# Odd transpose sets of the probabilities written to the output projection's PSUM bank, and one residual moved up in VectorE's order

## The chip, the cores and the metric
The kernel runs on one core of a Trainium2 chip. The metric is the time of one execution on the device in microseconds (us), median of several runs. Engines: TensorE (PE in the profile; its weight loads are PEld), VectorE (DVE), ScalarE (ACT), GpSimd (POOL), and SyncE (SP), which issues the DMAs. PSUM is `ps`, eight banks of 128 partitions by 512 fp32.

## The reference, cut to what matters
A layer norm of 2048 tokens of 128 features feeds two branches whose outputs are added to the input. One is a linear attention with a short convolution, done once. The other, nearly all of the time, has six layers; each is a windowed attention and a gated feed-forward part:

```python
for i in range(DEPTH):      # 6
    x = attn_layer(shift_tokens(x), Wqkv[i], q_scale[i], k_scale[i], Wo[i]) + x
    x = ffn_layer(shift_tokens(x), ln_g[i], ln_b[i], W1[i], b1[i], W2[i], b2[i]) + x
```

The attention has 16 heads of 64, l2-normed and rotated queries and keys, windows of 32 queries that see 64 keys, a softmax, and `out @ Wo`. The feed-forward part normalizes, computes two products with W1, multiplies one with the gelu of the other, and applies W2. `shift_tokens` makes half of the features come from the token before.

## The kernel before, in words
The tokens are cut into groups of 256, so that six layers by eight groups make 48 steps. Every step runs parts of three groups at once: `a_` parts (projections, norms and rotation of group m), `b_` parts (scores, softmax, attention of group m - 1) and `c_` parts (second output projection, feed-forward of group m - 2). All engines follow one list, `SCHEDULE` (L57): `run` (L75) goes through it once per step, and an engine executes the tokens that it has a part for. What one engine needs of another is a semaphore wait at the head of a part. Within an engine the order of the list is the order of the queue. From that list, around the change:

- TensorE: ... c_mu b_s3 c_var a_x2 a_y2 b_pt0 b_pt1 b_att0 b_att1 a_sp0 c_h0 a_sp1 b_wo a_x3 c_h1 b_pt2 a_y3 b_pt3 b_att2 c_h2 a_norm1 b_att3 c_down
- VectorE: ... b_scale1 b_max1 c_zn a_mx2 a_my2 b_sum1 a_kn0 c_hm0 a_kn1 a_mx3 c_hm1 a_my3 c_hm2 c_fin b_xb, then b_rcq and a_mx0 of the next step
- ScalarE: ... c_rs a_rh a_sqy2 b_pto0 c_zh b_pto1 a_sqx2 b_exp1 b_oto0 c_gelu0 c_gelu1 b_pto2 a_sqy3 a_sqx3 (in the last group of a layer the split of the next layer's weights) b_pto3 c_gelu2 b_oto1
- POOL: ... b_sub1 a_xl c_zl b_nrm1 a_rot2 a_rot3
- SyncE: per step the windows of V, the keys (L317, after a_kn1), the queries (L329, after a_rot3), the halo.

The probabilities of one group are two chunks of 128 tokens by 16 heads. `b_pt(n, i)` (L551) transposes one of four sets, four 128 by 128 transposes (L564) into bank `PTB`; `b_pto` (L1083) on ScalarE copies the bank into `PT`; `b_att(n, i)` (L567) multiplies with V. All four sets use the same bank, so each waits for the copy of the one before (`pts_done`).

Bank `WO` holds in turn: the output projection of chunk 0 (`b_wo`, L594), read by the residual `b_xb` (L892); in the next step that of chunk 1 (`c_wo`), read by `c_xb`; the centred activations (`c_mu`, L600), read by `c_zsq` and by `c_zn` (L898) on VectorE; and the variance. `out_proj` (L581) waits before it writes the bank: for `zn_done` with chunk 0, for `xb_done` with chunk 1. The next scores, `b_s(n, 0)` (L511), wait for the queries' DMA (`q_in`). Of the feed-forward part, `c_h(0)` (L608) waits for `zl_done` from POOL.

Of the kernel before, what the change touches and what calls it, by code (L numbers as in the profile page):

```python
# [17 lines left out]
P = 128  # L18
# [4 lines left out]
C = T // P  # L23
# [11 lines left out]
HQ = 4  # L35
# [18 lines left out]
PTB, WO, NORM, FF = 4, 5, 6, 7  # L54
# [4 lines left out]
    a_norm0 a_xl+1 w_h1 a_sqx1 b_exp0 c_xs c_zl a_rck c_mu w_l0 b_s3 c_var b_nrm1 c_zsq a_halo a_x2 a_lnk a_rot2  # L59
    c_rs a_rot3 a_y2 a_rh a_sqy2 b_pt0 b_pto0 b_scale1 b_pt1 c_zh b_att0 w_l2 b_max1 b_att1 a_sp0 b_pto1 a_sqx2  # L60
    c_h0 c_zn b_exp1 a_mx2 a_sp1 a_my2 b_oto0 c_gelu0 b_sum1 b_wo a_x3 c_wl c_gelu1 a_kn0 b_pto2 c_h1 b_pt2 c_hm0
    a_y3 a_kn1 a_mx3 a_sqy3 a_sqx3 b_pt3 c_hm1 c_wh b_att2 c_h2 a_norm1 w_h2 a_my3 c_hm2 b_att3 b_pto3 c_down
    c_gelu2 c_fin b_xb w_l1 b_oto1""".split()
LAG = {"w": 0, "a": 0, "b": 1, "c": 2}
EARLY = """a_xs0 a_xh0 a_xl0 a_halo0 a_v0 a_vs0 a_v1 a_vs1 a_x0 a_y0 a_mx0 a_my0 a_sqy0 a_sqx0 a_rot0
    a_x1 a_y1 a_mx1 a_my1 a_sqy1 a_sqx1 a_rot1 a_norm0 a_sum0 a_rck0 a_lnk0 a_rh0 a_rl0 a_sp0 a_sp1 a_kn0 a_kn1
# [65 lines left out]
def program(nc, a):  # L132

    with ExitStack() as ctx:
        def sb(name, shape, dt=F32):
            return ctx.enter_context(nc.sbuf_tensor(name, shape, dt))

        def sem(name):
            return ctx.enter_context(nc.semaphore(name))

        ps = ctx.enter_context(nc.psum_tensor("ps", [P, 8, 512], F32))
# [31 lines left out]
        E = sb("E", [P, C, HP, 2, KEYS])  # L173
        PT = sb("PT", [P, HP, P])
# [16 lines left out]
        ident = sb("ident", [P, P])  # L191
# [49 lines left out]
        s = {name: sem(name) for name in SEMS}  # L241
# [137 lines left out]
        def _(e):  # L379
            def mm(out, lhsT, rhs, start=True, stop=True, **kw):  # L380
                return e.matmul(out, lhsT, rhs, start=start, stop=stop, **kw)  # L381
# [9 lines left out]
            for g in range(G1):  # L391
                for c in range(C1):
                    e.wait_ge(s["xn_done"], g * C1 + c + 1)
                    ins = e.transpose(ps[:, g, c * P:(c + 1) * P], xn[:, g * C1 + c, :], ident[:, :])
# [156 lines left out]
            def b_pt(n, i):  # L551
                c = i // 2
                if i % 2 == 0:
                    e.wait_ge(s["pn_done"], n * C + c + 1)
                if n or i:
                    e.wait_ge(s["pts_done"], n * 4 + i)
                for h in range(HQ):
                    if i == 0 and h == 1:
                        e.wait_ge(s["e_done"], n * C + C)
                    if i == 1 and h == HQ - 1:  # L560
                        e.wait_ge(s["v2_in"], n * 256 + 256)
                    if i == 2 and h == 1:
                        e.wait_ge(s["ots_done"], n * 4 + 2)
                    ins = e.transpose(ps[:, PTB, h * P:(h + 1) * P], E[:, c, i % 2 * HQ + h, :, :], ident[:, :])  # L564
                ins.then_inc(s["pt_done"], 1)

            def b_att(n, i):  # L567
# [13 lines left out]
            def out_proj(n, c):  # L581

                if c == 0 and n % G == 0:
                    e.wait_ge(s["wo_in"], n // G * 16 + 16)
                if c:
                    e.wait_ge(s["xb_done"], n * C + 1)
                elif n:
                    e.wait_ge(s["zn_done"], n)
                e.wait_ge(s["ots_done"], n * 4 + 2 * c + 2)
                for h in range(HP):  # L590
                    ins = mm(ps[:, WO, 0:P], wo[:, h, :], OT[:, c, h, :], h == 0, h == HP - 1)
                ins.then_inc(s["wo_done"], 1)

            def b_wo(n, _):  # L594
                out_proj(n, 0)

            def c_wo(j, _):
                out_proj(j, 1)
# [77 lines left out]
            def m_out(g):  # L676
# [4 lines left out]
                for c in range(C1):  # L681
# [30 lines left out]
            m_out(3)  # L712

            run({"a_v": a_v, "a_x": a_x, "a_y": a_y, "a_norm": a_norm, "a_sp": a_sp, "b_rqt": b_rqt, "b_s": b_s, "b_pt": b_pt,
                 "b_att": b_att, "b_wo": b_wo, "c_wo": c_wo, "c_mu": c_mu, "c_var": c_var, "c_h": c_h,
                 "c_down": c_down}, tail)
# [238 lines left out]
        def _(e):  # L955
            def act(out, in_, f=ACT.Copy, **kw):
                return e.activation(out, in_, f, **kw)  # L957
# [125 lines left out]
            def b_pto(n, i):  # L1083
                e.wait_ge(s["pt_done"], n * 4 + i + 1)
                if i % 2 == 0 and (i or n):
                    e.wait_ge(s["o_done"], n * C + i // 2)
                act(PT[:, i % 2 * HQ:i % 2 * HQ + HQ, :], ps[:, PTB, :]).then_inc(s["pts_done"], 1)

            def b_oto(n, c):
                for i in range(2):  # L1090
# [39 lines left out]
            def m_den(g):  # L1130
                e.wait_ge(s["dn_done"], g + 1)
                if g:
# [18 lines left out]
            a_sqx(0, 2)  # L1151
            run({"w_h": w_h, "c_wh": c_wh, "a_xs": a_xs, "a_xh": a_xh, "a_halo": a_halo, "a_vs": a_vs, "a_sqy": a_sqy, "a_sqx": a_sqx,
                 "a_lnk": a_lnk, "b_lnq": b_lnq, "a_rh": a_rh, "b_exp": b_exp, "b_pto": b_pto, "b_oto": b_oto, "c_xs": c_xs,
                 "c_zsq": c_zsq, "c_rs": c_rs, "c_zh": c_zh, "c_gelu": c_gelu}, lambda g: None)

# [129 lines left out]
```

## Time and profile before

| what | us |
|---|---|
| median of 3 runs | 1779.91 (1777.05 to 1782.78) |
| the profiled execution's own time | 1762.38 |
| its span, first to last instruction | 1760.6 |
| TensorE matmuls, weight loads | 1601.1 (91%), 1298.7 (74%) |
| VectorE, ScalarE, POOL | 1228.2 (70%), 1153.2 (65%), 1003.2 (57%) |
| mean granted TensorE clock | 0.983 |

A busy share is a mean over the whole span. Matmuls overlap, so their busy time is not their work. The list of waits says which engine stood idle and what ended the idle time; the timeline shows single instructions, merged where they are alike, with the idle time before them in square brackets.

### The profile page before, as it was taken

Reading aid. Unit: us, or ns where it says so; the run is one execution under the profiler, and the core shown is the slowest. Engines: PE = TensorE matmul, PEld = TensorE weight load, DVE = VectorE, ACT = ScalarE, POOL = GpSimd, SP = SyncE. Lnnn points to the kernel's source line nnn. Section 1 sums busy time; section 2 is a strip of 40 time slices with the busy share of each in tenths; the row PEclk is TensorE's granted clock in tenths of the full one; section 3 lists DMA queues with packets and bytes.
Section 4 is the critical chain, followed back from the end, with each engine's and each line's share of the span. In section 5 each row is a group of like instructions: output and inputs, shape, how many; then the busy total and the mean of one; then the engine's idle time right before and its main releaser. Section 6 shows DMA issues by size and latency. Waiting matters only on the chain. (4 is left out here: it accounts for less than half of the span.)

```text
span 1760.6 us, 75862 instructions
## 1 busy us (share of the span) xinstructions
PE 1601.1 (91%) x33590; PEld 1298.7 (74%) x33590; DVE 1228.2 (70%) x1912; ACT 1153.2 (65%) x2115; POOL 1003.2 (57%) x757
## 2 busy tenths in 40 slices
PE   5879999989999999999999899999999999999976
PEld 4557778777777877877777777777778777777765
DVE  7666677677677667767767776776776777677662
ACT  2246676767767766776776666776676676767644
POOL 2155566666565756646666664675565586566551
PEclk9999999999999999999999999999999999999996
DMA  3266665675765567566567656657755666665650
GB/s 129 57 169 148 154 144 135 152 182 134 165 151 127 137 153 198 132 147 157 122 153 201 144 130 145 154 126 186 169 135 138 153 146 143 150 157 123 151 125 25
DMA packets 98568, 252.97 MB, mean 144 GB/s; under 512 B 30016, under 2 KB 36288, under 8 KB 97472
## 3 DMA queue, kind: packets, MB, share of 16 engines
q1 hardware_dynamic: 98240, 248.12, 59.0%
q8 instruction: 264, 4.33, 1.1%
q14 instruction: 64, 0.52, 0.1%
HBM read 44.59 MB, written 2.10 MB: 27 GB/s over the span
## 5 line engine op out<-in xcount | busy, mean ns | idle before, releaser
L805 DVE SCALAR_TENSOR_TENSOR UV<-ps,veca,rope 128x512 f32<-128x512 f32 x768 | 531.2, 744 | 184.5 <-PE ps L381 155.3
L1212 POOL TENSOR_TENSOR KK<-UV 128x512 f32<-128x512 f32 x192 | 241.9, 1282 | 406.6 <-DVE UV L805 403.4
L957 ACT ACTIVATE sq<-ps 128x512 f32<-128x512 f32 (+1 forms) x400 | 228.1, 583 | 263.0 <-PE ps L381 172.4
L1212 POOL TENSOR_TENSOR Qtb<-UV 128x512 f32<-128x512 f32 x192 | 242.9, 1287 | 86.5 <-DVE UV L805 86.5
L381 PE MATMUL ps<-xh,wh 128*128 128x256 f32 x768 | 245.1, 319 | 1.7 <-ACT sq L957 0.8
L1231 POOL TENSOR_TENSOR E<-E,ri 128x1024 f32<-128x1024 f32 x96 | 182.8, 1904 | 79.3 <-DVE ri L878 73.6
L381 PEld LDWEIGHTS ps<-PT,V 64*64 64x64 f32 x12288 | 194.1, 136 | 40.0 <-issue 35.4
L381 PE MATMUL ps<-xh,wl 128*128 128x256 f32 x768 | 218.0, 284 | 3.8 <-issue 3.8
L381 PE MATMUL ps<-xl,wh 128*128 128x256 f32 x768 | 217.7, 283 | 1.0 <-issue 1.0
L381 PE MATMUL ps<-PT,V 64*64 64x32 f32 x12288 | 210.3, 221 | 3.6 <-ACT PT L957 2.0
L1222 POOL TENSOR_TENSOR E<-E,mx 128x1024 f32<-128x1024 f32 x96 | 182.9, 1905 | 51.3 <-DVE mx L872 51.2
L381 PE MATMUL ps<-OT,wo 128*128 128x128 f32 x1536 | 197.2, 282 | 7.4 <-issue 7.2
L381 PEld LDWEIGHTS ps<-OT,wo 128*128 128x128 f32 x1536 | 183.6, 195 | 14.9 <-issue 8.8
L381 PEld LDWEIGHTS ps<-KK,Qtb 64*32 64x32 f32 x12288 | 133.3, 106 | 71.2 <-issue 41.3
L381 PE MATMUL ps<-KK,Qtb 64*32 64x64 f32 x12288 | 159.4, 227 | 28.5 <-DMA Qtb<-Qtb 18.6
L381 PEld LDWEIGHTS ps<-xh,wh 128*128 128x128 f32 x768 | 147.0, 191 | 30.0 <-ACT Vs L957 17.8
L957 ACT ACTIVATE hid<-ps,vecc 128x256 f32<-128x256 f32 x144 | 68.2, 473 | 150.9 <-PE ps L381 150.1
L866 DVE TENSOR_TENSOR E<-ps,rq 128x1024 f32<-128x1024 f32 x96 | 117.4, 1222 | 55.1 <-PE ps L381 54.9
L564 PE MATMUL ps<-ident,E 128*128 128x128 f32 x768 | 121.6, 281 | 37.2 <-ACT PT L957 36.1
L381 PEld LDWEIGHTS ps<-xh,wl 128*128 128x128 f32 x768 | 147.4, 192 | 3.4 <-issue 2.1
L381 PEld LDWEIGHTS ps<-xl,wh 128*128 128x128 f32 x768 | 147.0, 191 | 2.6 <-issue 2.6
L876 DVE TENSOR_REDUCE rs<-E 128x16 f32<-128x1024 f32 x96 | 117.1, 1220 | 40.5 <-ACT E L957 40.5
(128 smaller groups left out, 3106.0 us busy)
## 6 DMA issues: line engine op xcount, KB each, us to landing
V<-Vs SPq DMA_DIRECT2D x672, 128.0 KB
KK<-KK SPq DMA_DIRECT2D x384, 128.0 KB
Qtb<-Qtb SPq DMA_DIRECT2D x384, 128.0 KB, 2.4
rope<-in_c_rope SPq DMA_DIRECT2D x48, 512.0 KB, 4.1
raw<-in_Wqkv SPq DMA_DIRECT2D x6, 1536.0 KB, 7.9
V<-Vs SPq DMA_DIRECT2D x96, 64.0 KB
V<-V SPq DMA_DIRECT2D x96, 64.0 KB, 2.0
wo<-in_Wo SPq DMA_DIRECT2D x6, 512.0 KB, 6.5
```

What stands on the lines that cost most here:

```text
L381: return e.matmul(out, lhsT, rhs, start=start, stop=stop, **kw)
L564: ins = e.transpose(ps[:, PTB, h * P:(h + 1) * P], E[:, c, i % 2 * HQ + h, :, :], ident[:, :])
L805: e.scalar_tensor_tensor(UV[:, p % 2, slot, :].rearrange("p (i t) -> p i t", i=2), ps[:, half, :].rearrange("p (i t) -> p i t", i=2), veca ...
L866: e.tensor_tensor(E[:, c].rearrange("p j r k -> p r j k"), ps[:, 2:4, :].rearrange("p r (j k) -> p r j k", k=KEYS), by_row.unsqueeze(3).br ...
L876: e.tensor_reduce(rs[:, c], heads(E[:, c]), AX.X, ALU.add).then_inc(s["rs_done"], 1)
L957: return e.activation(out, in_, f, **kw)
L1212: e.tensor_tensor(dst, u, v, op).then_inc(s["rot_done"], 1)
L1222: e.tensor_tensor(ev, ev, mx[:, c].unsqueeze(2).broadcast_to([P, H, KEYS]), ALU.subtract).then_inc(s["sub_done"], 1)
L1231: e.tensor_tensor(ev, ev, ri[:, c].unsqueeze(2).broadcast_to([P, H, KEYS]), ALU.mult).then_inc(s["pn_done"], 1)
```

## The change
Sets 1 and 3 of the transposes are written to bank `WO` instead of `PTB`, and `b_pto` reads them there. Sets 0 and 2 wait only for their probabilities (the copy of the set before the last in `PTB` lies behind an attention part that waited for it). Set 1 waits for `zn_done`, the last reader of `WO` from the feed-forward part, and set 3 for `xb_done`, the residual of chunk 0. These two waits leave `out_proj`. For set 3 to find that residual done, `b_xb` moves in the list from behind `c_fin` to behind `a_kn1`; only VectorE has a part for it.

```diff
-    a_y3 a_kn1 a_mx3 a_sqy3 a_sqx3 b_pt3 c_hm1 c_wh b_att2 c_h2 a_norm1 w_h2 a_my3 c_hm2 b_att3 b_pto3 c_down
-    c_gelu2 c_fin b_xb w_l1 b_oto1""".split()
+    a_y3 a_kn1 b_xb a_mx3 a_sqy3 a_sqx3 b_pt3 c_hm1 c_wh b_att2 c_h2 a_norm1 w_h2 a_my3 c_hm2 b_att3 b_pto3 c_down
+    c_gelu2 c_fin w_l1 b_oto1""".split()
...
                 if i % 2 == 0:
                     e.wait_ge(s["pn_done"], n * C + c + 1)
-                if n or i:
-                    e.wait_ge(s["pts_done"], n * 4 + i)
+                elif i == 3:
+                    e.wait_ge(s["xb_done"], n * C + 1)
+                elif n:
+                    e.wait_ge(s["zn_done"], n)
...
-                    ins = e.transpose(ps[:, PTB, h * P:(h + 1) * P], E[:, c, i % 2 * HQ + h, :, :], ident[:, :])
+                    ins = e.transpose(ps[:, (PTB, WO)[i % 2], h * P:(h + 1) * P], E[:, c, i % 2 * HQ + h, :, :], ident[:, :])
...
-                if c:
-                    e.wait_ge(s["xb_done"], n * C + 1)
-                elif n:
-                    e.wait_ge(s["zn_done"], n)
                 e.wait_ge(s["ots_done"], n * 4 + 2 * c + 2)
...
-                act(PT[:, i % 2 * HQ:i % 2 * HQ + HQ, :], ps[:, PTB, :]).then_inc(s["pts_done"], 1)
+                act(PT[:, i % 2 * HQ:i % 2 * HQ + HQ, :], ps[:, (PTB, WO)[i % 2], :]).then_inc(s["pts_done"], 1)
```

## Rows read from the trace of the kernel before
**Rows 1.** The page, part 1: busy us, share of the span, instructions.
```profile
PE 1601.1 (91%) x33590; PEld 1298.7 (74%) x33590; DVE 1228.2 (70%) x1912; ACT 1153.2 (65%) x2115; POOL 1003.2 (57%) x757
```
**Rows 2.** Waits of the whole span: engine, line, releaser, us, times, longest.
```profile
PEld ps L381 <- issue: 141.7, 450, 3.7
PEld ps L564 <- ACT PT L957: 56.6, 96, 1.1
PEld ps L381 <- DMA Qtb<-Qtb: 29.7, 39, 3.7
```
**Rows 3.** Timeline, first pair: start, us, engine, line, operation, [idle before].
```profile
904.23 1.22 DVE L872 TENSOR_REDUCE mx<-E 128x16 f32<-128x1024 f32 x1
...
904.73 0.60 PE L564 MATMUL ps<-ident,E 128*128 128x128 f32 x4
...
905.37 0.47 DVE L902 SCALAR_TENSOR_TENSOR zs<-ps,vecc,zr 128x256 f32<-128x256 f32 x1
905.42 0.59 ACT L957 ACTIVATE PT<-ps 128x512 f32<-128x512 f32 x1
...
906.06 0.66 PE L564 MATMUL ps<-ident,E 128*128 128x128 f32 x4 [0.74 <-ACT PT L957]
...
906.76 0.59 ACT L957 ACTIVATE PT<-ps 128x512 f32<-128x512 f32 x1
```
**Rows 4.** Timeline of the last step: POOL's end and the transposes it releases.
```profile
1714.96 1.90 POOL L1231 TENSOR_TENSOR E<-E,ri 128x1024 f32<-128x1024 f32 x1 [2.71 <-DVE ri L878]
...
1716.92 1.12 PE L564 MATMUL ps<-ident,E 128*128 128x128 f32 x4
```
**Rows 5.** Timeline, behind the first pair: zl and the first matmul of c_h(0).
```profile
908.09 0.73 POOL L1226 TENSOR_TENSOR zl<-zs,zh 128x256 fp32r<-128x256 f32 x1
...
909.08 0.39 PE L381 MATMUL ps<-zh,w1h 128*128 128x256 f32 x1
```
**Rows 6.** Timeline, second pair: eviction of set 2, end of a_y3, set 3.
```profile
914.36 0.60 ACT L957 ACTIVATE PT<-ps 128x512 f32<-128x512 f32 x1
...
914.75 0.28 PE L381 MATMUL ps<-xl,wh 128*128 128x256 f32 x1
915.01 0.42 PEld L564 LDWEIGHTS ps<-ident,E 128*128 128x128 f32 x4 [0.18 <-ACT PT L957]
```
**Rows 7.** Timeline between the pairs: what leads to a_kn(1), and a_my(3).
```profile
907.73 1.06 ACT L957 ACTIVATE E<-E 128x1024 f32<-128x1024 f32 x1
...
908.78 1.09 ACT L957 ACTIVATE OT<-ps 128x512 f32<-128x512 f32 x2
...
910.41 2.05 PE L381 MATMUL ps<-OT,wo 128*128 128x128 f32 x16
...
911.70 0.48 DVE L909 SCALAR_TENSOR_TENSOR hid<-ps,vecc,hid 128x256 f32<-128x256 f32 x1
912.10 1.22 DVE L849 TENSOR_TENSOR KK<-ps,KK 128x1024 f32<-128x1024 f32 x1
...
915.70 1.41 DVE L805 SCALAR_TENSOR_TENSOR UV<-ps,veca,rope 128x512 f32<-128x512 f32 x2 [0.62 <-ACT sq L957]
```
**Rows 8.** The residual's line: duration ns min/median/max, first and last start.
```profile
L884 DVE TENSOR_TENSOR XB<-ps,XA x96: 279/282/294, 136.0 to 1739.1; 128x128 f32<-128x128 f32 x96
```
**Rows 9.** SyncE's timeline, keys and queries; below, line 337's time to landing.
```profile
913.34 5.74 SPq L326 DMA_DIRECT2D KK<-KK  x8
919.18 4.99 SPq L337 DMA_DIRECT2D Qtb<-Qtb  x8
...
DMA to landing us min/median/max: 2.3/2.4/4.0
```
**Rows 10.** Timeline, loads of b_s(0): a free step, and two held ones.
```profile
247.93 1.41 PEld L381 LDWEIGHTS ps<-KK,Qtb 64*32 64x32 f32 x128 [0.23 <-issue]
...
893.47 1.32 PEld L381 LDWEIGHTS ps<-KK,Qtb 64*32 64x32 f32 x128 [0.57 <-DMA Qtb<-Qtb]
...
1673.02 1.06 PEld L381 LDWEIGHTS ps<-KK,Qtb 64*32 64x32 f32 x102 [0.77 <-DMA Qtb<-Qtb]
```

## Prediction
> **What bounds the kernel now.** I read the shares of busy time first, then who waited for whom, then one step in order of time, then the same few landmarks in each of steps 1 to 45. The page gives TensorE matmuls 91% of the span [rows 1], so what counts is time in which TensorE holds nothing. The list of waits has three large kinds on the weight loads, which run ahead of the matmuls: 141.7 us of "issue", 56.6 us in 96 waits of the probability transposes on the ScalarE copy into PT, and 29.7 us in 39 waits for the DMA that spreads the queries [rows 2]. The 96 are two per step: set 1 behind the eviction of set 0, set 3 behind that of set 2. The change goes at these two.
>
> All times of a step below are of the step whose set 0 is evicted at 905.42; the others repeat it within 0.02 us unless said. Step length is 33.1 us in the quickest ones.
>
> **First pair.** Set 0 starts at 904.73 and takes 0.60. Its eviction runs from 905.42 to 906.01, and set 1 starts at 906.06, after 0.74 idle on the matmul side [rows 3]. After the change set 1 no longer waits for that eviction but for c_zn, the last reader of bank WO: 905.37 to 905.84 [rows 3]. From an end to a released TensorE row takes 0.06: a POOL operation ends at 1716.86 and its transposes start at 1716.92 [rows 4]. So set 1 starts at 905.84 + 0.06 = 905.90 in place of 906.06 here, 0.16 earlier. In this step c_zn is late; in steps 1 to 45 it ends 0.30 to 0.45 after the eviction's start (steps 2 and 8 aside, where it ends before that start), in most at 0.31, which gives 0.64 - 0.37 = 0.27. So the pair is not freed: the stall of 0.74 shrinks to about 0.5, for c_zn stands on VectorE right behind the 1.22 us maximum [rows 3], and that hangs on the last scores, which TensorE finished before a_x2 and a_y2.
>
> What is late next: ScalarE evicts set 1 from 906.76 in either kernel, because it is busy until then with c_zh, whose copy and bias sit between the two evictions; the attention of set 0 covers that. Behind the attention comes c_h(0), which waits for zl from POOL. It ends at 908.82 and c_h starts at 909.08 [rows 5]; it can't start before 908.88, so 0.20 is the most here. In two thirds of the steps zl ends 0.10 later against the same landmark and only 0.10 is left; in the others 0.23. The smaller of both limits, added over steps 1 to 45, is 6.4 us (0.14 a step), against 45 x 0.27 = 12 us if nothing but c_zn limited it and 0 if zl came 0.1 us later everywhere.
>
> **Second pair.** Set 2 is evicted from 914.36 to 914.96; the last matmul of a_y3 starts at 914.75, and set 3 starts at 915.01, 0.26 later, with 0.18 idle on the load side [rows 6]. An unheld row follows at 0.12 (the spacing of the neighbouring matmuls), so removal gives 0.26 - 0.12 = 0.14 to 0.15. The new wait of set 3 is on the moved residual: VectorE ends a_kn(1) at 913.32 [rows 7], the residual takes 0.28 [rows 8], so it is done by 913.6, 1.3 us before it is asked for. ScalarE's copy of set 2 ends at 914.96, before the attention asks (915.45). In the 5 steps that split a new layer's weights, the eviction of set 3 stands behind that work, and nothing is gained there: 40 x 0.15 = 6.0 us. Both pairs: 12.4 us on TensorE's own line.
>
> **The moved residual.** It comes out of VectorE's queue behind c_fin and goes in ahead of a_mx3; POOL's and SyncE's queues are not passed, and the keys' DMAs wait for a_kn(1), which stays ahead of it. Its matmuls end at 912.46, 0.86 before VectorE gets there [rows 7]. It pushes a_mx3 and c_hm(1) back by 0.20 to 0.28 (0.14 more with the copy of one column, in 18 steps). Cover: a_my3 starts after 0.62 idle [rows 7], so the rotation of the queries behind it isn't moved, and c_h(2) asks for c_hm(1) over 1 us after it is there. If that cover were gone it would cost 0.3 x 48 = 14 us. Where it left, VectorE then waits 3.2 us for a_x0, so nothing is won. Six waits a step become two on TensorE; I take 0, as transposes behind a satisfied wait follow at 0.12 like others. One such "issue" gap is at most 0.17, so the other end is 4 x 0.17 x 48 = 33 us gained, which I leave out: the output projections show no such gap.
>
> **Where the gain can be lost: the queries' DMA.** SyncE issues the keys' 8 DMAs from 913.34 (5.74 us), then the queries' 8 from 919.18 (4.99 us), each landing 2.4 us after its issue [rows 9]. The next b_s(0) needs the last one. Landing read as end of issue - 0.6 + 2.4 falls on the start of b_s(0) within 0.1 us in most steps. In 25 of the steps 1 to 45 the loads of b_s(0) sat idle beyond the 0.23 of a free one for it, 0.57 in one, 0.77 in another [rows 10]; in 20 they did not, with 0.03 to 0.9 us in hand (0.2 at the middle). So a faster TensorE just waits longer in 25 steps, unless the transfer starts sooner. It starts when a_kn(1) ends, 7.92 after the eviction of set 0 in all ordinary steps. That hangs on c_hm(0) at 911.70, which has two releasers within 0.04 us: a_kn(0) before it, and the gelu, reached by ScalarE through the exponential (907.73), then OT (908.78), then a table load [rows 7]. OT starts 0.01 before the exponential's recorded end, where unheld ScalarE rows start 0.10 before: so OT waits for the attention's end, and 0.09 can be given. a_kn(0) can give 0.10. So the keys start 0.09 earlier; the bounds are 0 (VectorE or ScalarE holds it) and 0.14 (all of the first pair). Where the queries were waiting for POOL's rotation instead (16 steps), they gain with a_y3, by the first pair.
>
> Step by step, smaller of (TensorE's gain) and (slack + transfer's gain): held steps 2.4 us, free steps 4.6 to 5.1, together 7.0 to 7.5; with no gain of the transfer 5.0; with no such limit 12.4. I take 6.8. The profiled run has a span of 1760.6 and a time of 1762.38; it would have 1755.6. The median of the runs is 17.5 above that run, and the difference is carried over: 1779.9 - 6.8 = 1773.1.
>
> The Trainium skill (Perfetto Trace Analysis, section What "DMA-bound" means) counts as DMA-bound a stretch in which the issuing engine's sequencer is solid with DMA slices. By that rule SyncE, solid here from 913.34 to 924.17, would set every step and the change would give nothing, 1779.9. The 20 free steps speak against it as a rule for all of them, the 25 held ones for it. The same page (Matmuls) wants independent groups in different banks so that evictions overlap; by that alone the sum would be 12.4.
>
> **Rivals.**
> (a) The transfer holds more of it: the keys' start doesn't move, and the steps with 0.2 in hand turn out held. Then 2 to 5 us remain: 1776 (1774.6 to 1780). For it: 25 steps held already, and a margin read only to 0.1. Chance 0.33.
> (b) The transfers come forward with everything, so that nearly all of 12.4 is kept: 1767.5. Against it: the fixed 7.92. Chance 0.12.
> (c) Slower: TensorE's pauses. Of the 141.7 us of "issue" [rows 2], 31 pauses of 0.45 us or more within the steps hold 32 us (mean 1.04), mostly between b_s(0) and b_s(3) while SyncE issues the windows of V. No operand is late there; they don't repeat from step to step, so place and number may change with every shift of the program. Each new one costs about 1 us. It needs 12 more of them to be slower by 5.3 us; 15 more give 1779.9 - 6.8 + 15.6 = 1788.7. Chance 0.09.
> (d) The swap does the opposite of what it says: c_zn comes later than the eviction it replaces. The point is an end later than 0.59 after the eviction's start; it is at 0.31 to 0.45 now, so 0.14 to 0.28 in hand. At 0.5 us later everywhere set 1 starts at 0.87 in place of 0.64, 0.23 x 45 = 10.4, less some 2.4 from the second pair: 1788. Chance 0.03.
>
> **How the numbers follow.** Forecast 0.43 at 1773.1 (own range 1770 to 1774.6). A change is told from none from 0.3%, 5.3 us, that is below 1774.6 or above 1785.2. Faster: 0.43 + 0.12 = 0.55. Same: 0.33. Slower: 0.09 + 0.03 = 0.12. The range reaches from a little under (b), 1765.5, to 1783, which takes in (a) and the runs' own scatter of 3 us and leaves (c) and (d) out.
>
> **What would show it.** Right: set 1 starting about 0.37 to 0.5 after the eviction of set 0 starts, released by VectorE; set 3 at 0.12 behind a_y3; the transposes' waits on PT gone and about 15 to 25 us of waits on c_zn in their place; more or longer waits of b_s(0) on the queries' DMA than 29.7 us; the keys' issue at 7.83. Wrong: c_zn ending after 0.59; VectorE's idle time before a_my3 gone; the issue pauses far from 32 us; waits of b_s(0) unchanged.

## The result, and the profile after

The changed kernel is faster by a little under one per cent. All comparisons are of runs on the same chip in alternation, each ratio with its 95% interval.

| | before | after |
|---|---|---|
| median of 15 runs each, us | 1771.53 | 1753.81 |
| lowest to highest | 1754.4 to 1782.78 | 1748.93 to 1766.29 |
| ratio after / before | | 0.9923 [0.9901, 0.9945] |
| profiled execution, span | 1762.38, 1760.6 | 1766.29, 1764.5 |

0.9923 is 13.6 us on 1771.5 (9.7 to 17.5). The forecast was 6.8 us. The two profiled executions would say the opposite, 3.9 us slower: that of after is the slowest of its 15 runs, that of before (1762.38) is shorter than 12 of the 15 runs of before. (The medians differ by 17.7; the ratio, taken over runs that stand beside each other, is what I go by.) With a spread of 17 to 28 us inside one kernel, a span tells nothing about 13 us; the landmarks of the steps do, which repeat to a few hundredths.

The page after, part 1 (busy us, share of the span, instructions), against [rows 1]:

```profile
PE 1603.1 (91%) x33590; PEld 1308.3 (74%) x33590; DVE 1226.0 (69%) x1912; ACT 1147.8 (65%) x2115; POOL 1002.6 (57%) x757
```

The same waits as in [rows 2], after (engine, line, releaser: us, times, longest):

```profile
PEld ps L381 <- issue: 147.4, 453, 3.7
...
PEld ps L381 <- DMA Qtb<-Qtb: 35.4, 40, 3.7
PEld ps L566 <- DVE zs L900: 34.2, 46, 1.1
...
PE ps L566 <- DVE zs L900: 22.9, 45, 0.7
```

The 96 waits on the ScalarE copy are gone. In their place are 46 on c_zn, 34.2 us on the load side and 22.9 on the matmul side (I had said 15 to 25), and the queries' DMA holds 35.4 us in place of 29.7.

Timeline, first pair, against [rows 3] (start, us, engine, line, operation, [idle before]); this step's set 0 is evicted at 911.38:

```profile
911.33 0.47 DVE L900 SCALAR_TENSOR_TENSOR zs<-ps,vecc,zr 128x256 f32<-128x256 f32 x1
911.38 0.59 ACT L955 ACTIVATE PT<-ps 128x512 f32<-128x512 f32 x1
...
911.86 0.66 PE L566 MATMUL ps<-ident,E 128*128 128x128 f32 x4 [0.57 <-DVE zs L900]
...
914.04 0.73 POOL L1224 TENSOR_TENSOR zl<-zs,zh 128x256 fp32r<-128x256 f32 x1
...
914.92 0.39 PE L381 MATMUL ps<-zh,w1h 128*128 128x256 f32 x1
```

Set 1 starts 0.48 after the eviction of set 0, where it was 0.64, and 0.06 after c_zn's end at 911.80. c_h(0) starts 3.54 after the eviction, where it was 3.66 [rows 5], with zl ended 0.15 before.

Timeline, second pair, against [rows 6], with the residual (L882) in its new place:

```profile
919.07 0.28 DVE L882 TENSOR_TENSOR XB<-ps,XA 128x128 f32<-128x128 f32 x1
...
920.21 0.60 ACT L955 ACTIVATE PT<-ps 128x512 f32<-128x512 f32 x1
...
920.60 0.28 PE L381 MATMUL ps<-xl,wh 128*128 128x256 f32 x1
...
920.72 0.60 PE L566 MATMUL ps<-ident,E 128*128 128x128 f32 x4
920.92 1.09 ACT L955 ACTIVATE sq<-ps 128x512 f32<-128x512 f32 x2
921.25 0.85 PEld L381 LDWEIGHTS ps<-PT,V 64*64 64x64 f32 x52 [0.17 <-issue]
```

Set 3 stands 0.12 behind a_y3, as forecast, and lasts 0.60 where the held one of [rows 6] is recorded with 0.66:

```profile
915.01 0.66 PE L564 MATMUL ps<-ident,E 128*128 128x128 f32 x4
915.60 0.41 PE L381 MATMUL ps<-PT,V 64*64 64x32 f32 x13
```

That is before. The attention followed 0.59 behind set 3's start there and follows at 0.53 now. This 0.06 was not in my sum.

SyncE's timeline after, against [rows 9], and the next b_s(0), here a free one:

```profile
919.18 4.96 SPq L326 DMA_DIRECT2D KK<-KK  x8
924.94 4.95 SPq L337 DMA_DIRECT2D Qtb<-Qtb  x8
```

```profile
932.15 1.32 PEld L381 LDWEIGHTS ps<-KK,Qtb 64*32 64x32 f32 x128 [0.23 <-issue]
```

The keys' first issue is 7.80 after the eviction of set 0, where it was 7.92.

The same landmarks, medians over the ordinary ones of steps 1 to 45, read from the timeline as start after the eviction of set 0:

| landmark | before | after | gain |
|---|---|---|---|
| set 1 | 0.64 | 0.37 to 0.51 | |
| c_h(0) | 3.66 | 3.55 | 0.11 |
| keys' first issue | 7.92 | 7.80 | 0.12 |
| first product of a_y3 | 8.68 | 8.56 | 0.12 |
| set 3 | 9.60 | 9.36 | 0.24 |
| attention of set 2 | 10.20 | 9.88 | 0.32 |
| mask ahead of b_s(0) | 20.77 | 20.45 | 0.32 |

0.12 comes from the first pair and 0.20 from the second; nothing between the attention and the mask takes any of it back. What decides from there is whether the queries have landed.

### The profile page after: what moved, and what is told of

Same layout as the page of the kernel before. It is cut to its first block and busy times, and to the rows that moved or that the text cites. A ratio compares the mean times of both kernels' runs of the same rounds, so it can differ in the third digit from the quotient of the medians.

```text
span 1764.5 us, 75677 instructions
## 1 busy us (share of the span) xinstructions
PE 1603.1 (91%) x33590; PEld 1308.3 (74%) x33590; DVE 1226.0 (69%) x1912; ACT 1147.8 (65%) x2115; POOL 1002.6 (57%) x757
## 5 line engine op out<-in xcount | busy, mean ns | idle before, releaser
L381 PEld LDWEIGHTS ps<-PT,V 64*64 64x64 f32 x12288 | 199.1, 137 | 45.0 <-issue 38.6
L381 PE MATMUL ps<-PT,V 64*64 64x32 f32 x12288 | 215.7, 222 | 8.0 <-issue 5.0
L381 PEld LDWEIGHTS ps<-OT,wo 128*128 128x128 f32 x1536 | 186.4, 198 | 14.7 <-issue 8.6
L566 PE MATMUL ps<-ident,E 128*128 128x128 f32 x768 | 119.0, 278 | 27.1 <-DVE zs L900 22.9
```

Source lines behind the costliest of these rows:

```text
L566: ins = e.transpose(ps[:, (PTB, WO)[i % 2], h * P:(h + 1) * P], E[:, c, i % 2 * HQ + h, :, :], ident[:, :])
```

## The experiments

**The changed kernel again**, to see whether the gain repeats.

> The changed kernel once more, beside the kernel before on the same chip. The first theory (the queries' DMA holds back half of TensorE's gain, 6.8 us of 12.4) expects a ratio of 0.996; that nothing holds it (the full 12.4 on TensorE's line) expects 0.993; that the profiled execution of before was a quick one, and an ordinary one has more to lose to waits and pauses, expects 0.992 or less. In the trace the landmarks of a step (set 1 at 0.38 to 0.51 after the first eviction starts, c_h(0) at 3.55, set 3 at 9.36, the keys' issue at 7.80) should stand as in the first profile; only the pauses and the waits for the queries' DMA should differ.

Measured 1755.83 against 1766.29 in 35 runs: 0.9942 [0.9917, 0.9966]. Its span was 1748.7, 15.8 us from the other profile of the same program, and its landmarks were the same. The gain repeats, at 10.2 us; a gain of 9.7 to 14.7 us lies in both intervals. That leaves out the forecast's 6.8 us only with the first comparison; the interval of the second holds both 0.996 and 0.993.

**First pair alone.** Set 1 goes to `WO`, set 3 stays:

```diff
-                if n or i:
+                if i == 1:
+                    if n:
+                        e.wait_ge(s["zn_done"], n)
+                elif n or i:
...
-                    ins = e.transpose(ps[:, PTB, h * P:(h + 1) * P], E[:, c, i % 2 * HQ + h, :, :], ident[:, :])
+                    ins = e.transpose(ps[:, WO if i == 1 else PTB, h * P:(h + 1) * P], E[:, c, i % 2 * HQ + h, :, :], ident[:, :])
```

> Only set 1 goes to the output projection's bank; set 3 stays in the transposes' bank behind the eviction of set 2, the residual stays at the end of the step. TensorE's own line is 6.4 us shorter, and the keys' issue 0.12 earlier in each step. DMA-hold theory: 3 to 4.5 us, ratio about 0.998. No hold: 6.4 us, 0.9965. If the excess over the forecast comes from the earlier keys' issue (all of a step after it is moved), this kernel has most of the whole gain: 0.994.

1760.81, ratio 0.9973 [0.9945, 1.0001], 4.8 us. The keys' first issue stands at 7.79 after the eviction of set 0 (median of steps 1 to 45). The interval takes in 0.998 and 0.9965 and leaves out 0.994, so the first pair doesn't have most of the gain.

**Second pair alone**, with the residual moved (`WO if i == 3`, the wait for `xb_done` at set 3):

> Only set 3 goes to the output projection's bank, with the residual moved up; set 1 stays behind the eviction of set 0. TensorE's own line is 6.0 us shorter, behind the keys' issue, so the transfer does not move. DMA-hold theory: only the steps with slack gain, 2 to 3 us, ratio 0.9985. No hold: 6.0 us, 0.9966. If an early residual itself were worth something, more than that.

1764.58, ratio 0.9993 [0.9964, 1.0023]. **The residual's move alone** (`b_xb` behind `a_kn1` in the list, nothing else):

> The kernel before with only the residual of chunk 0 moved from behind c_fin to behind a_kn(1) in VectorE's queue; banks and waits as before. All theories that rest on the landmarks expect no difference, ratio 1.000 within 0.002, as a_my(3) starts behind 0.6 us of idle time. If moving the residual is a part of the gain, 0.997 or less.

1765.76, ratio 1.0004 [0.9976, 1.0033]. The waits of the three, of the first pair alone:

```profile
PEld ps L381 <- issue: 149.7, 458, 3.7
...
PEld ps L567 <- DVE zs L903: 33.5, 44, 1.3
...
PEld ps L381 <- DMA Qtb<-Qtb: 27.7, 32, 3.7
```

of the second pair alone:

```profile
PEld ps L381 <- issue: 142.9, 449, 3.7
...
PEld ps L566 <- ACT PT L957: 47.0, 48, 1.1
...
PEld ps L381 <- DMA Qtb<-Qtb: 37.3, 41, 3.5
```

and of the move alone:

```profile
PEld ps L381 <- issue: 147.7, 460, 3.7
PEld ps L564 <- ACT PT L957: 56.5, 96, 1.1
...
PEld ps L381 <- DMA Qtb<-Qtb: 30.0, 34, 3.8
```

The move costs nothing that can be told and leaves the waits on PT and on the queries as they were. The first pair brings the keys' issue forward with it, and the queries' wait doesn't grow. The second pair takes 9.6 us of waits on PT away on the load side (56.6 to 47.0), can't move the keys' issue, which precedes it, and the wait for the queries grows by 7.6 us. Its time alone is 1.2 us below before, with an interval from 6.4 faster to 4.1 slower: the 9 us by which its landmarks come earlier (0.20 in 45 steps) lie outside.

**The kernel before, again**, to see how far two sets of runs and two profiles of one program lie apart:

> The kernel before against itself: ratio 1.000, and the width of its interval is what such a comparison can tell. Its trace is a second profile of before. If the first profile was typical, b_s(0) is held for the queries' DMA by about 15 us in all (26 steps) and what is left of the steps without holds and without TensorE's long pauses is 1520 us. If the excess of the measured gain lies in holds that ordinary runs of before have and its first profile had not, the holds are well over 15 us here.

1771.87 against 1772.69: 0.9998 [0.9971, 1.0024]. Its span was 1773.0, 12.4 from the other profile of the same program; its wait for the queries was 31.7 us in place of 29.7. So the surplus of the gain over the forecast doesn't lie in holds that the first profile of before lacked.

**Half the transfers.** From the second step on, every other one of the keys' and queries' DMAs is left out, in the kernel before, in after, and with the second pair alone. The waits for these transfers are set to the smaller count:

```diff
-                for hq in range(HQ):
+                for hq in range(0, HQ, 2) if m else range(HQ):
```

> The kernel before with only half of the keys' and queries' DMAs from the second step on (4 of 8 each; the other heads keep the first step's data). The queries land about 2.4 us earlier, so b_s(0) is never held: holds fall from 15 us to near 0. If the hold is all that the transfer costs, ratio 0.991. If fewer DMAs also take TensorE's pauses away, 0.98.

> The changed kernel with the same half of the DMAs left out. DMA-hold theory: without holds the whole 12.3 us of TensorE's line are kept, so this stands 12.3 us below the light kernel before (0.7% of it). The rival, that the change gains elsewhere too (more than its landmarks move), expects 15 us or more; if the holds take nothing in either kernel, the difference is the same as with all DMAs, 12 us, and both light kernels stand equally far below their full ones.

1752.3 and 1732.57: 0.989 [0.9852, 0.9928] and 0.9786 [0.9747, 0.9825] of before. Repeated on another chip beside the second pair alone:

> The kernel before with half of the keys' and queries' DMAs left out (as e6), again, as the base for the next two on one chip. Ratio 0.989 as the first time; by the first profile's holds alone 0.991.

> Only set 3 moved (as e3), with half of the keys' and queries' DMAs left out. With all DMAs this part alone gave about nothing, 1 us, though it takes 0.20 us a step from TensorE's line. Transfer theory: the hold ate it, so without holds 0.20 x 45 = 9 us show, 0.5% below e10. If instead the second pair is worth nothing to the end for another reason (a wait on another engine behind it), it stays within 2 us of e10.

> The changed kernel with the same DMAs left out (as e7), again. TensorE's line is 0.32 us a step shorter than before, so 14 us, 0.8% below e10 and 5 us below e11. The first pair of runs stood 18 us apart; if that repeats, the change gives more than TensorE's line shows.

| half the transfers | us | ratio to before |
|---|---|---|
| order of before | 1753.54 | 0.9884 [0.984, 0.9927] |
| second pair alone | 1745.93 | 0.9832 [0.9787, 0.9877] |
| both pairs | 1729.33 | 0.9764 [0.9719, 0.9809] |

The waits with half the transfers and the second pair alone, where only the first step's wait for the queries and one more are left:

```profile
PEld ps L381 <- issue: 141.7, 472, 3.7
...
PEld ps L566 <- ACT PT L957: 46.8, 48, 1.0
...
PEld ps L381 <- DMA Qtb<-Qtb: 3.9, 2, 3.7
```

0.9832 less 0.9884 is 0.52%, 9 us, for a change that gave 0.07% with all transfers. 0.20 in each of 45 steps is 9.0 us. The two intervals overlap, so the time alone would not carry this; with the waits of both kernels it does: the queries' DMA is what takes the second pair's gain. Halving the transfers does one more thing: TensorE's long pauses (below) are 15 to 19 in these five profiles, against 19 to 29 in the nine with all transfers. So the time between before and its own half-transfer kernel is not the hold alone.

Both pairs give 1.2% here (21 us), and 1.04% (18 us) in the first comparison, where the landmarks account for 0.32 x 45 = 14 us. The surplus of 4 to 7 us is not in the ordinary steps. In steps without a long pause and at full granted clock, the median length is 33.21 us in the order of before and 32.93 with both pairs, in both comparisons: 0.28 x 45 = 12.6 us. What differs is the granted clock of the runs:

| half the transfers, mean of the runs | granted clock | time x clock, us |
|---|---|---|
| order of before, two comparisons | 0.9823, 0.9808 | 1721.6, 1720.9 |
| second pair alone | 0.9830 | 1715.6 |
| both pairs | 0.9858, 0.9862 | 1709.5, 1708.4 |

Time x clock is my estimate of the time at full clock. Within one kernel it is near: over 34 runs of before, a run is 0.8 us longer for each us of time x (1 - clock). By it the two pairs give 12.1 and 12.5 us and the second pair 5.3, about what their landmarks show. With all transfers the same estimate gives 10.4 us for both pairs, 3.9 for the first and 1.3 for the second (each within some 2 us). Why the clock is higher in the quickest kernel is not shown.

**The low part of the activations earlier.** After, with `a_xl+1` ahead of `a_rl` on POOL, so that `zl` of the same step is ready sooner:

> The changed kernel with the low part of the next group's activations (a_xl, 0.73 us on POOL) moved from behind b_sub(1) to ahead of a_rl, into POOL's idle 0.7 us there. zl then ends 0.7 us earlier, and c_h(0) no longer stands at zl's end but starts with TensorE's line: at 3.42 after the first eviction's start in place of 3.47 to 3.57. Limit by zl: 0.05 to 0.15 us a step on TensorE's line, 4 to 6 us, and less after holds: ratio to before 0.990 to 0.992. If it is not zl that holds c_h(0), no change from the changed kernel, 0.9932.

1760.98, 0.9944 [0.9916, 0.9972]: no gain over after that can be told. Its landmarks did move, by half of what was expected: zl ends 2.81 after the eviction of set 0 in place of 3.49, c_h(0) starts at 3.47 in place of 3.54 (3.42 expected), and the attention of set 2 at 9.82 in place of 9.88 (medians). So zl did hold c_h(0), and 0.07 x 45 = 3 us is too little for these intervals. Its waits on the queries' DMA were 36.8 us.

**The keys earlier.** After, with VectorE's a_kn1 ahead of c_hm0; on TensorE set 2 goes ahead of c_h1, on ScalarE its eviction ahead of c_gelu1:

```diff
-    c_h0 c_zn b_exp1 a_mx2 a_sp1 a_my2 b_oto0 c_gelu0 b_sum1 b_wo a_x3 c_wl c_gelu1 a_kn0 b_pto2 c_h1 b_pt2 c_hm0
-    a_y3 a_kn1 b_xb a_mx3 a_sqy3 a_sqx3 b_pt3 c_hm1 c_wh b_att2 c_h2 a_norm1 w_h2 a_my3 c_hm2 b_att3 b_pto3 c_down
+    c_h0 c_zn b_exp1 a_mx2 a_sp1 a_my2 b_oto0 c_gelu0 b_sum1 b_wo a_x3 c_wl a_kn0 b_pto2 c_gelu1 b_pt2 c_h1
+    a_y3 a_kn1 c_hm0 b_xb a_mx3 a_sqy3 a_sqx3 b_pt3 c_hm1 c_wh b_att2 c_h2 a_norm1 w_h2 a_my3 c_hm2 b_att3 b_pto3 c_down
```

> The changed kernel with three neighbours swapped, so that the keys' scaling a_kn(1) comes ahead of c_hm(0) in VectorE's queue, and set 2's transposes and eviction ahead of c_h(1) and c_gelu(1) on TensorE and ScalarE. a_kn(1) then ends at about 7.40 after the first eviction's start in place of 7.77, and the keys' issue starts there. TensorE's line keeps its length (c_h(1) gets its operand at 7.9 and asks at 8.1). Transfer theory (after the change the start of the keys' issue sets most steps): holds fall by up to 0.4 us in the steps where the queries' issue stands behind the keys', not where it stands behind POOL's rotation at 13.55; about 5 us in all, ratio to before 0.990. If TensorE's line alone sets the time now, no change from the changed kernel, 0.993.

1752.29 against 1773.98: **0.9872 [0.9833, 0.991]**, the lowest ratio of a kernel with all its transfers. Its keys' issue, the eviction of set 0 of the same step, and its waits:

```profile
903.38 4.96 SPq L326 DMA_DIRECT2D KK<-KK  x8
```

```profile
895.98 0.59 ACT L955 ACTIVATE PT<-ps 128x512 f32<-128x512 f32 x1
```

```profile
PEld ps L381 <- issue: 148.6, 457, 4.5
...
PEld ps L566 <- DVE zs L900: 34.3, 45, 1.3
...
PEld ps L381 <- DMA Qtb<-Qtb: 27.7, 30, 3.7
```

The keys start 7.40 after the eviction in place of 7.80, and the wait for the queries falls from 33.0 and 35.4 us (two profiles of after) to 27.7. Whether it beats after itself is not settled: 0.9872 against 0.9923 and 0.9942, with intervals that overlap those of after.

## Why the prediction was right or wrong

For each profile I cut the stretch from step 0 to step 46 in three: what b_s(0)'s loads sat idle for the queries' DMA beyond a free 0.23 to 0.33; the load side's "issue" pauses of 0.55 us or more; and the rest.

| us, one profile each | DMA hold (steps) | pauses (number) | rest |
|---|---|---|---|
| before, two profiles | 15.0 (26), 16.7 (29) | 27.6 (23), 36.8 (28) | 1520.0, 1521.4 |
| residual's move alone | 16.1 (25) | 31.4 (23) | 1520.3 |
| after, two profiles | 20.0 (28), 18.0 (29) | 39.3 (29), 28.6 (19) | 1507.6, 1507.8 |
| first pair alone | 13.8 (21) | 34.2 (24) | 1515.8 |
| second pair alone | 21.2 (32) | 32.6 (25) | 1514.3 |
| after, keys earlier | 14.5 (24) | 36.1 (29) | 1505.8 |

The rest is steady within 1.4 us here; the pauses move by 9 to 11 us between profiles of one program. The rest also takes in what a lowered clock costs, and is not always so steady: the order of before with half the transfers has 1538.3 and 1529.7 in its two profiles, at a granted clock of 0.986 and 0.992 in that stretch. From the mean of the first three, 1520.6, the rest falls by 12.9 us, and the hold takes about 3 of it back.

- **First pair, 0.14 a step.** Right. c_zn releases set 1, zl limits c_h(0), and 0.12 is gained. The rest of the first pair alone falls by 4.8 us; I had 6.4.
- **Second pair, 0.15 a step.** Mis-sized: 0.20. The held set also ran 0.06 longer than a free one; I counted only its later start. 0.05 more in 40 to 45 steps is 2.0 to 2.3 us. The rest falls by 6.3 us with it alone.
- **The moved residual, 0.** Right (1.0004, and a rest of 1520.3).
- **Six waits become two, 0.** Right; the gap ahead of the attention stays at 0.17 <-issue.
- **The keys' issue, 0.09 earlier (0 to 0.14).** Near: 0.12. It follows the whole of the first pair.
- **The queries' DMA takes 5.6 of 12.4.** This step of the sum failed: the mechanism holds, its size doesn't. Both parts alone show the mechanism (27.7 against 37.3 us of waits), and halving the transfers frees the second pair. But in after the hold grew by only some 3 us, from 15.9 to 19.0, means of three and two profiles (1.3 to 5.0 between single ones, so this is rough). With 0.32 x 45 = 14.4 gained on TensorE's line, that leaves 11.3 us, inside 9.7 to 17.5 of the first comparison and beside 10.2 of the second. The keys' start, which I moved by 0.09, moved by 0.12. With it, my way of summing gives at most 25 x 0.12 = 3.0 us in the held steps and 20 x 0.32 = 6.4 in the free ones, 9.4 in all.
- **Rivals.** (a), the transfer holds more: fallen for the change as a whole, true for the second pair alone. (b), nearly all is kept: its number, 12.4 us, is the nearest to the measured 10 to 14, but the transfer still holds 28 or 29 steps; what was missing in the sum was the second pair's length. (c) did not come as a cost: pauses of 39.3 and 28.6 us after, 27.6 and 36.8 before. Their places did change, as it said (below). (d) did not come: c_zn ends 0.31 to 0.45 after the eviction's start, as before.
- **The level, 17.5 above the profiled run.** This step failed too, and by more: it was carried over from three early runs. Over 15 runs the median of before is 1771.53, 9.2 above the profiled run, so the forecast stood 8.4 too high from the start. That is 8.4 of the 19.3 us between 1773.1 and 1753.81. The other 10.9 are gain that I did not forecast (17.7 by the medians less 6.8): 4.1 is how far the medians' 17.7 goes beyond the 13.6 of runs side by side, 2.0 the second pair, some 2.5 the hold, and the last 2.3 lie within the intervals.

The rule of the Trainium skill (Perfetto Trace Analysis, section What "DMA-bound" means), from which I drew that nothing would be gained, does not hold for this kernel as a whole: 28 or 29 of the 46 steps of after are held and time is still gained, because the transfer's start moves with TensorE's first pair and the other steps don't wait for it.

Open: with all transfers the landmarks (14.4) and the rest (12.9) agree, but the size of the hold is known only by single profiles. Why the granted clock differs between the kernels with half the transfers is not known, and no run took all pauses away.

## What to carry to other kernels

Before counting a stall on the busiest engine as gain, look where the transfer that the next stage needs is issued: a stall ahead of the issue moves both and is kept, a stall behind it is given back in every step that the transfer holds. Take a held operation's whole cost from the start of what follows it, not from its own start. And where runs of one program differ by more than the change is worth, compare landmarks within the steps of both traces and the medians of many runs, never two spans.

## What the runs showed of the hardware

**Pauses that no operand explains, and the clock with them.** These are the pauses of rival (c). One in after, on the matmul side, between the first and the second transpose of set 0; scores, probabilities and V were all there by the timeline (POOL's last write to E ended at 393.74, the next piece of V is asked for only by set 1):

```profile
394.67 0.27 PE L566 MATMUL ps<-ident,E 128*128 128x128 f32 x1
398.09 0.98 PE L566 MATMUL ps<-ident,E 128*128 128x128 f32 x7 [3.16 <-issue]
```

The windows around it (stretch, length, PE busy and instructions, granted clock, DMA share, GB/s):

```profile
390.00:398.00 8.00, 4.94 (x128) 1.00 1.00 227
398.00:402.00 4.00, 3.66 (x119) 0.71 0.67 150
402.00:406.00 4.00, 2.82 (x37) 0.50 0.04 10
406.00:412.00 6.00, 6.00 (x38) 0.67 0.15 34
```

A granted clock of 0.50 is the lower of the two levels, 1.2 GHz. The step that begins right behind this pause, with the eviction of set 0 at 398.68, has another pause of 2.64 us in it and took 41.6 us where 33.5 is usual. The same step in the changed kernel's second profile has the same second pause, ran at full granted clock (0.84 on average in the first profile), and took 35.0. The 6.6 us between the two go with the clock: 41.6 x (1 - 0.84) is 6.7.

**They stand at fixed places of TensorE's instructions.** I numbered TensorE's recorded instructions (loads, matmuls and the sequencer's own) in order of time and took the place of every "issue" pause of 0.55 us or more between steps 0 and 46. In the 14 profiles, 293 of 313 pauses stand at one place of every 256 instructions (number 193 or 194, counted from 0, of each run of 256). These steps have some 250 such places in a profile, and 15 to 29 pauses. Which of them pause repeats with the order of TensorE's instructions: 17 of 23 pauses of before stand at the same weight load in its second profile, 14 of 19 of the changed kernel's second profile in its first, 15 of 17 between the two profiles with both pairs and half the transfers; but only 3 of 23 between before and after, whose lists for TensorE differ by the waits and the banks. So a pause goes with the place in the list of instructions and not with an operand.

**They end a fixed time after a packet of instructions.** The DMA view of after lists, beside the kernel's own transfers, a queue of kind "instruction" (queue and kind: packets, MB, share of 16 engines), first for the whole span, then for 394 to 399 us, the stretch of the pause above:

```profile
q8 instruction: 263, 4.31, 1.1%
...
q8 instruction: 1, 0.02, 1.7%
```

Each of these packets has 16384 bytes, and there is about one for every 256 recorded instructions of TensorE. The one of that stretch ran from 395.36 to 396.69, and TensorE went on at 398.09, 1.40 later. In the pause of 4.46 us below, the packet ended at 929.71 and the loads went on at 931.12, 1.41 later. Over all 313 pauses the median is 1.45 us, and nine in ten lie between 1.26 and 1.77, where packets come some 6 us apart. So by their place and by this timing the pauses are waits for TensorE's own instructions. Why some packets come too late is not shown: those that end a pause take about as long (1.1 us) as the others.

Their length varies. At one load of step 23 the changed kernel pauses 1.72 us in its first profile and 4.46 in its second. The window of the longer one, and the one behind it:

```profile
925.00:931.00 6.00, 1.81 (x69) 0.96 1.02 219
931.00:937.00 6.00, 5.88 (x35) 0.50 0.66 142
```

The DMA engines were fully busy in both stretches shown (1.00 and 1.02). That is not the rule: in the 313 pauses they were busy 0.70 on average, a quarter of them under 0.48, against 0.61 in the us ahead of those places where nothing paused. Fewer transfers went with fewer pauses (15 to 19 against 19 to 29), so the DMA traffic may play a part in what comes late; it is not shown.

**One operation held is more than late.** The four transposes last 0.60 unheld and 0.66 behind a wait, and the next loads follow at 0.53 and 0.59 behind their start.
